# Two attention layers on one core: the output projection's nine products take turns with a projection unit's nine

## The reference

```python
# layer 0
q, k, v = split_heads(x @ Wq + bq), split_heads(x @ Wk + bk), split_heads(x @ Wv + bv)
scores = q @ k.T / sqrt(32) + beta * adj            # masked where adj <= 0
x = layernorm(x + softmax(scores) @ v)
# layer 1
q, k, v = x @ Wq.T, x @ Wk.T, x @ Wv.T + bv         # in heads
a = softmax(q @ k.T * 384 ** -0.5 + adj)
x = layernorm(x + (a @ v) @ Wo.T + bo)
```

## Time and profile before

| | |
|---|---|
| Time, median of 3 runs | 1110.51 us (1110.2 to 1111.41) |
| The profiled execution: time, span | 1112.23 us, 1110.4 us |
| TensorE matmul busy | 1063.3 us, 96% |
| VectorE, GpSimd, ScalarE busy | 85%, 48%, 41% |
| Products of `ps_u` and `ps_o` (L366) on the chain that ended last | 53% and 9% of the span |

### The profile page before, as it was taken

How to read it: one execution, slowest core, us unless ns; L and a number is a source line. 1 busy time by engine, 2 the same in 40 slices (tenths; PEclk the granted TensorE clock), 3 DMA queues, 4 the chain that set the end, 5 groups by cost and what they waited for, 6 DMA issues and landing times.

```text
span 1110.4 us, 38177 instructions
## 1 busy us (share of the span) xinstructions
PE 1063.3 (96%) x16896; PEld 920.9 (83%) x16896; DVE 940.4 (85%) x1641; ACT 449.8 (41%) x712; POOL 531.2 (48%) x454
## 2 busy tenths in 40 slices
PE   4799999999999999999999999999999999998875
PEld 3688888888888888888888888888888888887765
DVE  4756989899898989989898998989889898987855
ACT  4334444343444434344343443444344443434321
POOL 0424545555454554545455454544546454455522
PEclk9899999999999999999999999999999999999988
DMA  8020211102021010212102021210202121010000
GB/s 267 19 77 2 71 37 57 39 16 82 26 68 40 31 55 26 76 33 69 32 12 80 26 76 33 68 33 10 82 26 75 34 68 33 9 45 26 16 16 30
DMA packets 61684, 53.31 MB, mean 48 GB/s; under 512 B 35920, under 2 KB 55376, under 8 KB 61520
## 3 DMA queue, kind: packets, MB, share of 16 engines
q1 hardware_dynamic: 60320, 49.10, 14.5%
q10 hardware_dynamic: 1200, 1.77, 0.4%
HBM read 38.28 MB, written 12.58 MB: 46 GB/s over the span
## 4 chain that ended last, share of the span: by engine, by line
PE 90%; DVE 5%; issue 2%; DMA 1%; POOL 1%; ACT 1%; SPq 0%; POOLq 0%; DVEq 0%; ACTq 0%
PE ps_u L366 53%; PE ps_s L382 9%; PE ps_o L366 9%; PE ps_p L444 7%; PE ps_p L459 7%; PE ps_x L396 3%; PE ps_o L473 2%; DVE row_sum L684 1%; DMA k_sb<-in_wk 1%; DVE probs L636 1%; DMA xt_in<-in_x_t 1%; DVE row_max L647 1%; DVE xt_lo L664 0%; POOL probs L777 0%; POOL probs L783 0%
## 5 line engine op out<-in xcount | busy, mean ns | idle before, releaser
L777 POOL TENSOR_TENSOR probs<-probs,row_max 128x768 f32<-128x768 f32 x128 | 209.5, 1637 | 297.8 <-DVE row_max L647 297.8
L783 POOL TENSOR_TENSOR probs<-probs,row_inv 128x768 f32<-128x768 f32 x128 | 190.6, 1489 | 128.7 <-DVE row_inv L692 68.5
L532 ACT COPY probs_t<-ps_p 128x768 f32<-128x768 f32 x128 | 102.8, 803 | 203.7 <-PE ps_p L444 203.7
L684 DVE TENSOR_REDUCE row_sum<-probs 128x12 f32<-128x768 f32 x128 | 121.6, 950 | 29.6 <-ACT probs L566 28.6
L366 PE MATMUL ps_u<-w_hi_v,xt_lo 128*128 128x384 f32 x384 | 138.4, 361 | 0.0
L796 POOL TENSOR_TENSOR rstd<-var_eps,minus_half 128x1 f32<-128x1 f32 x128 | 70.3, 549 | 140.2 <-DVE var_eps L728 140.2
L366 PE MATMUL ps_u<-xt_hi,w_lo_q 128*128 128x512 f32 x288 | 123.2, 428 | 11.4 <-DVE w_lo_q L620 11.4
L566 ACT ACTIVATE probs<-probs 128x768 f32<-128x768 f32 x128 | 108.6, 848 | 58.9 <-POOL probs L777 58.9
L366 PE MATMUL ps_u<-w_hi_v,xt_hi 128*128 128x384 f32 x384 | 129.9, 338 | 0.0
L366 PE MATMUL ps_u<-w_lo_v,xt_hi 128*128 128x384 f32 x384 | 129.6, 338 | 0.0
L647 DVE TENSOR_REDUCE row_max<-probs 128x12 f32<-128x768 f32 x128 | 121.4, 949 | 2.2
(11 more groups left out here) (66 smaller groups left out, 2029.4 us busy)
## 6 DMA issues: line engine op xcount, KB each, us to landing
xt_in<-in_x_t SPq DMA_DIRECT2D x16, 768.0 KB, 7.8
x_in<-in_x SPq DMA_DIRECT2D x16, 768.0 KB, 4.6
out<-z SPq DMA_DIRECT2D x64, 192.0 KB, 1.9
adj<-in_adj SPq DMA_DIRECT2D x64, 128.0 KB, 4.5
q_sb<-in_wq ACTq DMA_DIRECT2D x1, 576.0 KB, 6.7
k_sb<-in_wk ACTq DMA_DIRECT2D x1, 576.0 KB, 8.4
v_sb<-in_wv ACTq DMA_DIRECT2D x1, 576.0 KB, 11.2
q_sb<-in_wq SPq DMA_DIRECT2D x1, 576.0 KB, 10.7
```

The source lines that it names most:

```text
L532: nc.scalar.copy(probs_t[:].rearrange("p (a i) n -> p a (i n)", a=2), ps_p[:, :, 0:KT * P]).then_inc(probs_t_ready, 1)
L684: nc.vector.reduce_sum(row_sum[p][:], probs[p][:].rearrange("p i b k -> p (i b) k"), AX_X)\
L777: nc.gpsimd.tensor_tensor(s, s, over_keys(row_max[p]), ALU.subtract).then_inc(shifted, 1)
L783: nc.gpsimd.tensor_tensor(s, s, over_keys(row_inv[p]), ALU.mult).then_inc(probs_ready, 1)
```

## The change

When the tile `last` is one of layer 1 and the step has a unit, one function issues both. It makes the unit's first three products, then waits for what the result needs, and from there the result's and the unit's products take turns, in different banks (`ps_o` and a bank of `ps_u`). At the end three products of the result are left. The counts of products and of semaphore steps are as before; the semaphore of the unit is raised at its last product, the fifteenth of the eighteen in place of the ninth.

```diff
+            def unit_and_result(unit, tile):
+
+                await_unit(unit)
+                for n in range(3):
+                    unit_product(unit, 0, n)
+                await_result(tile)
+                for g in range(1, KT):
+                    for n in range(3):
+                        result_product(g - 1, n)
+                        last = unit_product(unit, g, n)
+                last.then_inc(unit_made, 1)
+                for n in range(3):
+                    last = result_product(KT - 1, n)
+                last.then_inc(o_made, 1)
...
             def step(cur, prev, last, done, turned, units, t, extra):
...
-                for unit in units[:1]:
-                    make_unit(unit)
-                if last:
-                    result(last)
+                if last and last[0] == 1 and units:
+                    unit_and_result(units[0], last)
+                else:
+                    for unit in units[:1]:
+                        make_unit(unit)
+                    if last:
+                        result(last)
```

More of the change, by code:

```diff
@@ L360, in _ @@
         def _(pe):
[L361 to L368, removed]
             def scores(tile):
@@ L397, in turn_activations, with await_unit @@
                 last.then_inc(xt_made, 1)
-            def make_unit(unit):
+            def await_unit(unit):
                 layer, ch, k = unit
@@ L414, in make_unit @@
                     pe.wait_ge(w_lo_ready, w_names.index(w) + 1)
-                bank = k % 2
-                if kind == "v":
[L417 to L422, removed]
-                else:
[L424 to L429, removed]
@@ L430, in make_unit, with unit_product @@
-                last.then_inc(unit_made, 1)
+            def unit_product(unit, g, n):
+                layer, ch, k = unit
+                kind, part = UNITS[k]
+                w = f"{kind}{layer}"
+                cols = slice(part * P, (part + 1) * P)
+                act_side = (xt_hi, xt_lo, xt_hi)[n][layer] if kind != "v" else (xt_lo, xt_hi, xt_hi)[n][layer]
+                w_side = (w_lo, w_hi, w_hi)[n][w] if kind != "v" else (w_hi, w_lo, w_hi)[n][w]
+                start, stop = g == 0 and n == 0, g == KT - 1 and n == 2
+                if kind == "v":
+                    return nc.tensor.matmul(ps_u[:, k % 2, 0:D], act_side[:, g, cols], w_side[:, g, :],
+                                            start=start, stop=stop)
+                return nc.tensor.matmul(ps_u[:, k % 2, :], w_side[:, g, cols], act_side[:, g, :],
+                                        start=start, stop=stop)
@@ new lines, in result_product, with make_unit @@
+            def result_product(g, n):
+                o_side, w_side = (o_lo, o_hi, o_hi)[n], (w_hi, w_lo, w_hi)[n]["o1"]
+                return nc.tensor.matmul(ps_o[:, 0:D], o_side[:, g, :], w_side[:, g, :],
+                                        start=(g == 0 and n == 0), stop=(g == KT - 1 and n == 2))
+            def make_unit(unit):
+                await_unit(unit)
+                for g in range(KT):
+                    for n in range(3):
+                        last = unit_product(unit, g, n)
+                last.then_inc(unit_made, 1)
@@ new lines, in await_result @@
+            def await_result(tile):
+                layer, ch, t = tile
+                if not (known(ch) and at(tile) == 0):
+                    pe.wait_ge(z_ready, at(tile))
+                pe.wait_ge(o_t_ready, at(tile) + 1)
+                if layer == 1:
+                    pe.wait_ge(o_lo_ready, TILES * number(ch) + t + 1)
+            def unit_and_result(unit, tile):
+                await_unit(unit)
+                for n in range(3):
[4 more added lines that the diff above has]
+                        result_product(g - 1, n)
+                        last = unit_product(unit, g, n)
+                last.then_inc(unit_made, 1)
+                for n in range(3):
+                    last = result_product(KT - 1, n)
+                last.then_inc(o_made, 1)
@@ L432, in turn_probs, with result @@
+            def result(tile):
+                await_result(tile)
+                if tile[0] == 0:
+                    for g in range(KT):
+                        last = nc.tensor.transpose(ps_o[:, g * P:(g + 1) * P], o_t[:, g, :], ident[:])
+                else:
+                    for g in range(KT):
+                        for n in range(3):
+                            last = result_product(g, n)
+                last.then_inc(o_made, 1)
             def turn_probs(tile):
@@ L464, in heads @@
                 last.then_inc(heads_made, 1)
[L466 to L479, removed]
             pe.wait_ge(ident_ready, 1)
```

## The result

The changed kernel takes 1127.38 us (median of 4 runs, 1126.77 to 1129.04), and the kernel before takes 1110.38 us beside it (median of 4 runs, 1110.20 to 1111.41). The ratio is 1.0151, with a 95% interval of [1.0139, 1.0163]. The profiled execution has a span of 1126.1 us against 1110.4.

What follows compares the result with a forecast made beforehand. TensorE, busy 96% of the span, was taken to bound the kernel. Waits of 13.5 us over 14 periods plus 2.4 us at the end, 15.9 us on a median of 1110.51, gave 1126.4 us, range 1120 to 1131.

Steps and rivals of the forecast that it cites:

- The wait costs its lateness, 0.14 to start and 0.07 behind it: TensorE's moved wait for `o_lo`: each late operand costs lateness + 0.21 us.
- Two steps of four are late, and the other two are not: Phase Y step 2 loses 0.59 us, phase X step 0 0.37; phase Y step 3 and phase X step 1 nothing.
- VectorE does not catch up: In the steady part VectorE's lateness arises anew each period, so each wait adds in full, 0.96 us a period.
- The 13.5 us for 14 periods: Steady part: waits for `o_lo` in two steps of four, 0.96 us a period, summed over 14 periods.
- In order, so the ready products stand too: TensorE's queue: six ready unit products stand behind the waiting one; rival that the wait is covered, about 1110.5 us, chance 0.05.
- Turns are free: Products alternating between two banks in the changed blocks: a change of bank gives and costs nothing, taken as zero.
- +67 us: Rival that turns cost: 0.09 us at all twelve changes of 62 blocks, 1193 us; chance 0.09 for over 0.01 us each.
- The rival that turns pay the fixed 0.011 us of a product: Turned products in 62 blocks lose a fixed 0.011 us each, gaining 8.2 us, for 1118.2 us; chance 0.08.
- The unit's later semaphore costs nothing: The unit's semaphore, 1.06 us later for ScalarE, costs nothing; if ScalarE ran late, `heads` waits 1.06 us at most.
- The end: Last two chunks, six blocks: waits add 2.4 us, 1.4 at one place and about 0.5 twice; bounds 0 and 3.6.
- my 15.9: Whole kernel: predicted total loss in us, 13.5 in the steady periods plus 2.4 at the end.
- What the profile would show: TensorE waits for `o_lo` some 33 times, about 12 us; period about 66.4 us; gaps about 0.5 and 0.3 us.

Runs made afterwards that it cites:

- the late pair alone: The change made only for tiles 0 and 2 of a chunk, the others as in the kernel before: 1129.89 us, 1.0159 of before.
- the timely pair: The change made only for tiles 1 and 3 of a chunk, the others as in the kernel before: 1112.78 us, 1.0008 of before.
- e1_wait_early: Against the changed kernel: same early wait after three unit products, but no turns, six unit products then nine result products; 1127.19 us, 1.0134 of before.
- e5_turns_low_last: Against the changed kernel: all turns kept, the result's three `o_lo` products and their wait put last; 1111.97 us, 0.9998 of before.
- e2_turns_late: Against the changed kernel: six unit products ahead of the wait in place of three, only three pairs take turns; 1111.76 us, 1.0000 of before.
- e6_plain_low_last: Against the kernel before: no turns, the result's `o_lo` products and their wait put last; 1109.01 us, 0.9977 of before.
- e9_turns_in_threes: All turns with `o_lo` products last, but groups of three products take turns in place of single ones; 1109.77 us, 0.9984 of before.

## Why the prediction was right

The forecast was 1126.4 us and the time is 1127.38. The steps, one by one:

- **The wait costs its lateness, 0.14 to start and 0.07 behind it.** In the changed kernel they are 0.14 and 0.08 us. Step 2 of phase Y lost 0.59 us (0.59 forecast), step 0 of phase X 0.37 (0.37).
- **Two steps of four are late, and the other two are not.** Shown by the split: 0.98 us a period with the late pair alone, 0.05 with the timely pair.
- **VectorE does not catch up.** The loss came in each of the twelve periods read, and the earlier `o_lo` on VectorE took 0.72 of the 1.02 us away. The 13.5 us for 14 periods were 14 x 1.02 = 14.3.
- **In order, so the ready products stand too.** The early wait without turns shows a unit's product that waits for `o_lo`. The rule of the Trainium skill that the prediction weighed (PSUM — Partial Sum Buffer, section "Engine vs sequencer instructions") holds here.
- **Turns are free.** Nearly. I took zero between -8.2 and, as a rival, +67 us; the measured price is 0.07 us a period (the change against the early wait) to 0.16 (the pair with `o_lo` last), 1 to 2 us in all. That is the 0.06 us a period by which 0.96 was too small. The rival that turns pay the fixed 0.011 us of a product is refuted by the twelve turned products of one width at 0.1733 us. So the 11 ns are no price of adding to the same bank. Two widths meet in 44 of the 62 blocks, not in 46, since 18 units and not 16 make v.
- **The unit's later semaphore costs nothing.** Nearly so at the least. The kernel with all turns and `o_lo` last raises it as late as the change does, and its whole period is 0.13 us longer than before. So this term is at most that.
- **The end.** I took 2.4 us with bounds of 0 and 3.6. The rows give 4.6 us for one period and the end, so 3.6, at the upper bound. The waits are about 2.1 us of it, near the forecast. Where TensorE waited before, the end of one `o_lo` was 6.45 us from the next (1049.64 to 1056.09) and is now 7.84 (1061.89 to 1069.73), 1.39 more, for which I had taken 1.4. The next block adds 0.6. The wait at 1103.71 adds nothing, since the next `o_lo` follows 7.22 us after the last in both kernels. The other 1.5 us are a lower granted clock, which my sum left out. The rows are below.
- **How near the sum came.** I was 0.8 us short in the periods and 1.2 us at the end. In the profiled executions a start that was 2.1 us earlier hides both: the spans differ by 15.7 us, against my 15.9. The medians differ by 17.0. That the forecast is within 1.0 us of the median is in part luck.
- **What the profile would show.** I said 33 waits and 12 us; it shows 20 and 10.7. In phase X step 0 the gap in starts is 0.29 us beyond the usual, but the row of the matmul before it lasts until 0.12 us ahead of it, and no wait is put down in these 14 steps. The period was to be 66.4 us, and it is 66.47.

The wait of the end that adds the most, in the changed kernel, with six of the unit's products still undone:

```profile
1062.04 0.41 PE L424 MATMUL ps_o<-w_hi_o,o_lo 128*128 128x384 f32 x1 [1.39 <-DVE o_lo L726]
```

Three stretches of the end that hold the same products in both kernels, and no wait for `o_lo` that is longer in one of them, in windows (the clock is the third number from the right), before and after:

```profile
1074.99:1079.17 4.18, 3.25 (x102) 2.75 (x103) 2.18 (x4) 2.01 (x3) 1.47 (x1) 0.60 0.01 4
1079.17:1083.98 4.81, 4.81 (x23) 4.78 (x19) 3.91 (x7) 0.00 (x0) 2.19 (x2) 0.64 0.00 0
1102.41:1105.33 2.92, 2.74 (x9) 2.26 (x9) 0.38 (x1) 0.00 (x0) 0.00 (x0) 0.62 0.18 67
```

```profile
1089.26:1094.10 4.84, 3.90 (x102) 3.25 (x102) 2.78 (x6) 2.03 (x3) 1.47 (x1) 0.50 0.01 3
1094.10:1099.25 5.15, 5.15 (x22) 5.12 (x19) 3.31 (x5) 0.00 (x0) 2.94 (x2) 0.59 0.00 0
1117.58:1120.98 3.40, 3.22 (x9) 2.74 (x9) 0.39 (x1) 0.00 (x0) 0.00 (x0) 0.50 0.16 58
```

Together they take 11.91 us before and 13.39 after, 1.5 us more, and in each the granted clock is lower after, so that a larger share ran at 1.2 GHz in place of 2.4. These are one execution of each kernel. Whether the change brings the lower clock about is not shown.

## What to carry to other kernels

When two independent streams are woven on an engine that works in order, each takes over the other's waits: compare the end of the late operand with the place where its first user will stand, in every step of the period, before moving anything. If one operand is late, put its products last and keep the ready ones first; here that alone gave 0.23%, with no weaving, all of it at the end of the program. Alternating PSUM banks between products brought nothing: 384-column products came every 0.1733 us with turns and without.

## What the runs showed of the hardware

Where TensorE waited for `o_lo`, the weight load started 0.11 to 0.12 us after VectorE's instruction ended and the product 0.14 to 0.15 us after it, in all 20 waits of the changed kernel and all 3 of the kernel before. The next product came 0.07 to 0.08 us later than in a flowing block, save for the last wait of the changed kernel, where the granted clock was 0.50 and the next product came after 0.45 us.

The start of the program differs from one profiled execution to the next with nothing changed there: the first residual sum started between 45.67 us (e1_wait_early) and 48.81 us (e5_turns_low_last). In the stretch from 20 to 70 us the granted clock was 0.86 before and 0.97 after the change, so different shares of it ran at 1.2 GHz in place of 2.4. The clock need not be all of it, since the latest start, of e5_turns_low_last, had 0.90 in this stretch. The windows of before, then of after:

```profile
20.00:70.00 50.00, 39.08 (x528) 31.84 (x527) 33.83 (x51) 20.83 (x30) 16.07 (x13) 0.86 0.13 38
```

```profile
20.00:70.00 50.00, 38.59 (x543) 31.80 (x542) 34.60 (x55) 21.76 (x32) 17.47 (x15) 0.97 0.17 51
```

A period read over twelve repeats leaves the start and the end out. In the four kernels that should have no wait and little or no price of turns (before, e2_turns_late, e6_plain_low_last and e9_turns_in_threes) it lies between 65.43 and 65.46 us, so a difference of 0.05 us can be told, where whole times differ by 1 us and more.
